# Cross attention: causal zeros set by GpSimd after the exponentials instead of mask products before them

## The reference, cut to what matters

```python
q = (Q @ wq.T).reshape(b, s, H, DH).transpose(0, 2, 1, 3)
k = (K @ wk.T).reshape(b, s, H, DH).transpose(0, 2, 1, 3)
v = (V @ wv.T).reshape(b, s, H, DH).transpose(0, 2, 1, 3)
att = jnp.einsum('bhqd,bhkd->bhqk', q, k) / jnp.sqrt(jnp.float32(DH))
causal = jnp.tril(jnp.ones((s, s), dtype=bool))
att = jnp.where(causal[None, None], att, -jnp.inf)
p = jax.nn.softmax(att, axis=-1)
out = jnp.einsum('bhqk,bhkd->bhqd', p, v)
```

## Time and profile before

| what | us |
|---|---|
| median of 3 runs | 2042.75 |
| lowest, highest | 2038.22, 2046.46 |
| span of the profiled execution | 2047.7 |
| busy in it: TensorE | 1796.9 (88%) |
| TensorE's weight loads | 1598.2 (78%) |
| VectorE | 1181.8 (58%) |
| ScalarE | 987.0 (48%) |
| GpSimd | 461.0 (23%) |
| exponentials of the cross attention, first to last start | 504.3 to 837.6 |

### The profile page before, as it was taken

The page is one execution under the profiler, slowest core; times in us unless marked ns, Lnnn a source line. Parts: engine busy times, 40 slices in busy tenths (PEclk is TensorE's granted clock), DMA queues, the critical chain, the costliest instruction groups (busy, mean ns, idle before and its releaser), DMA issues. The chain is left out here.

```text
span 2047.7 us, 39500 instructions
## 1 busy us (share of the span) xinstructions
PE 1796.9 (88%) x14845; PEld 1598.2 (78%) x14940; DVE 1181.8 (58%) x2467; ACT 987.0 (48%) x1964; POOL 461.0 (23%) x747
## 2 busy tenths in 40 slices
PE   2699999967999999578859969959999999999998
PEld 2577777756788887445549969959999999999998
DVE  2466677643676767388856869823444444444443
ACT  1367776641555555455546746623333333333331
POOL 3633443001011111134426845400000000000000
PEclk9899999986999999779979989979999999999999
DMA  5765666507877775260000033030000000000000
GB/s 165 161 142 122 132 136 140 105 25 161 178 166 161 162 161 105 91 228 1 0 1 1 1 106 97 24 117 6 10 20 10 10 10 20 10 10 10 10 16 11
DMA packets 104548, 155.87 MB, mean 76 GB/s; under 512 B 13120, under 2 KB 84800, under 8 KB 100416
## 3 DMA queue, kind: packets, MB, share of 16 engines
q1 hardware_dynamic: 99296, 149.95, 30.4%
q10 hardware_dynamic: 5120, 4.20, 1.1%
HBM read 107.97 MB, written 49.81 MB: 77 GB/s over the span
## 5 line engine op out<-in xcount | busy, mean ns | idle before, releaser
L2130 ACT ACTIVATE ffn_slots<-ps,ffn_sh 128x256 f32<-128x256 f32 x256 | 107.5, 472 | 322.7 <-PE ps L2036 322.4
L2036 PE MATMUL ps<-ffn_uT_hi,h 128*128 128x256 f32 x1024 | 245.5, 283 | 2.4 <-DVE ffn_uT_lo L2190 2.4
L2036 PE MATMUL ps<-ffn_uT_lo,h 128*128 128x256 f32 x1024 | 245.3, 283 | 0.0
L2036 PE MATMUL ps<-ffn_gT_lo,ffn_h 128*128 128x256 f32 x1024 | 243.9, 282 | 0.0
L2036 PE MATMUL ps<-ffn_gT_hi,ffn_h 128*128 128x256 f32 x1024 | 243.8, 282 | 0.0
L2036 PEld LDWEIGHTS ps<-ffn_uT_hi,h 128*128 128x128 f32 x1024 | 193.9, 189 | 2.6 <-DVE ffn_uT_lo L2190 2.6
L2036 PEld LDWEIGHTS ps<-ffn_uT_lo,h 128*128 128x128 f32 x1024 | 193.9, 189 | 0.0
L2036 PEld LDWEIGHTS ps<-ffn_gT_hi,ffn_h 128*128 128x128 f32 x1024 | 192.8, 188 | 0.0
L2036 PEld LDWEIGHTS ps<-ffn_gT_lo,ffn_h 128*128 128x128 f32 x1024 | 192.8, 188 | 0.0
L641 ACT ACTIVATE cross_probs<-ps 128x512 f32<-128x512 f32 x192 | 115.3, 602 | 108.7 <-PE ps L451 70.7
L641 ACT ACTIVATE latent_probs<-ps 128x512 f32<-128x512 f32 x192 | 115.4, 602 | 99.4 <-PE ps L451 55.9
(11 more groups left out here) (432 smaller groups left out, 5334.7 us busy)
## 6 DMA issues: line engine op xcount, KB each, us to landing
latent_split<-latent_qk_hi SPq DMA_DIRECT2D x16, 512.0 KB, 3.1
latent_split<-latent_qk_lo SPq DMA_DIRECT2D x16, 512.0 KB, 4.2
queries<-latent_split SPq DMA_DIRECT2D x32, 256.0 KB, 4.8
keys<-latent_split SPq DMA_DIRECT2D x32, 256.0 KB, 6.4
cross_split<-cross_qk_hi SPq DMA_DIRECT2D x16, 512.0 KB, 3.1
cross_split<-cross_qk_lo SPq DMA_DIRECT2D x16, 512.0 KB, 4.3
queries<-cross_split SPq DMA_DIRECT2D x32, 256.0 KB, 5.1
keys<-cross_split SPq DMA_DIRECT2D x32, 256.0 KB, 6.4
```

The source lines that it names most:

```text
L2036: last = nc.tensor.matmul(out_ap, a, b, start=start and n == 0, stop=stop and n == 1, **kw)
L2130: last = nc.scalar.activation(slots[:, p % 2, a], halved(HIDDEN_BANK + p % 2)[:, a, :], ACT.Gelu, scale=scales[:, 2 * p + a:2 * p + a + 1])
```

## The change

In the cross attention alone (`first=False`):

- `key_scores` no longer opens with the mask product; its own products start the accumulation. `query_scores` keeps its masks, so the maxima are taken over the same entries as before.
- GpSimd gets `bound_probs(i, g)`, two `affine_select` operations of 128x512 elements, in place on `probs`: the first, after the exponentials of step B, on the four diagonal 128x128 blocks of steps A and B, the second, after those of step C, on the four blocks of step C. Where the query's index is below the key's, zero is written, else the element is kept. Each counts `bounded` up.
- `weigh` waits for `bounded` instead of `ring_used`.
- GpSimd's queue in a slot becomes: `bound_probs(s - 1, 3)`, `split_context(s + 3)`, `bound_probs(s, 0)`, `row_statistics(s - 2)`, `bound_probs(s, 1)`, `bound_probs(s, 2)`.

In the diff, GpSimd's work of the first attention is only written in another way; its order there is the same.

```diff
--- before.py
+++ after.py
@@ -312,7 +312,7 @@
         q_raw, q_hi, k_raw, k_hi, qk_ready = sem("q_raw"), sem("q_hi"), sem("k_raw"), sem("k_hi"), sem("qk_ready")
         values_raw, values_ready = sem("values_raw"), sem("values_ready")
         scored, max_taken, max_split, turned, ring_used = sem("scored"), sem("max_taken"), sem("max_split"), sem("turned"), sem("ring_used")
-        shifted, weighed, evacuated = sem("shifted"), sem("weighed"), sem("evacuated")
+        shifted, weighed, evacuated, bounded = sem("shifted"), sem("weighed"), sem("evacuated"), sem("bounded")
         out_turned, normed, mixedT_raw, mixedT_hi, mixedT_ready = sem("out_turned"), sem("normed"), sem("mixedT_raw"), sem("mixedT_hi"), sem("mixedT_ready")
         latent_raw, latent_act, latent_ready = sem("latent_raw"), sem("latent_act"), sem("latent_ready")
         rope_raw, rope_biased, exchanged, roped_ready, roped_act = sem("rope_raw"), sem("rope_biased"), sem("exchanged"), sem("roped_ready"), sem("roped_act")
@@ -440,15 +440,17 @@
                     b = SECOND_RING + n % 2
                     q, k = queries[i % 3], keys[i % 3]
                     if step == "C":
-                        nc.tensor.matmul(quarters(b), ident16[:], masks[:, 1], start=True, stop=False, skip_group_check=True)
+                        if first:
+                            nc.tensor.matmul(quarters(b), ident16[:], masks[:, 1], start=True, stop=False, skip_group_check=True)
                         for m in range(4):
                             p, a = 2 * g + m // 2, m % 2
-                            last = nc.tensor.matmul(quarters(b)[:, m, :], k[:, p, a, P:S], q[:, p, P:S], start=False, stop=True, skip_group_check=True)
+                            last = nc.tensor.matmul(quarters(b)[:, m, :], k[:, p, a, P:S], q[:, p, P:S], start=not first, stop=True, skip_group_check=True)
                     else:
                         p = 2 * g + "AB".index(step)
-                        nc.tensor.matmul(halved(b)[:, :, 0:P], ident16[:], masks[:, 1, 0:2], start=True, stop=False, skip_group_check=True)
+                        if first:
+                            nc.tensor.matmul(halved(b)[:, :, 0:P], ident16[:], masks[:, 1, 0:2], start=True, stop=False, skip_group_check=True)
                         for a in range(2):
-                            last = nc.tensor.matmul(halved(b)[:, a, :], k[:, p, a, 0:P], q[:, p, :], start=False, stop=True, skip_group_check=True)
+                            last = nc.tensor.matmul(halved(b)[:, a, :], k[:, p, a, 0:P], q[:, p, :], start=not first, stop=True, skip_group_check=True)
                     last.then_inc(shifted, 1)
 
                 def turn_maxima(i, half):
@@ -463,7 +465,10 @@
                 def weigh(i, g):
 
                     q = QUADS * i + g
-                    pe.wait_ge(ring_used, ring["C", i, g] + 1)
+                    if first:
+                        pe.wait_ge(ring_used, ring["C", i, g] + 1)
+                    else:
+                        pe.wait_ge(bounded, 2 * q + 2)
                     if g == 0:
                         pe.wait_ge(values_ready, i + 1)
                     if q >= 2:
@@ -825,6 +830,14 @@
                     rows = core.X[:, i, :].rearrange("p (t d) -> p t d", d=D)
                     nc.gpsimd.tensor_tensor(rows, rows, b_out[:].to_broadcast([P, TT, D]), ALU.add).then_inc(x_biased, 1)
 
+                def bound_probs(i, g):
+                    q = QUADS * i + g
+                    two_heads = probs[:, q % 2, 0:2, :].rearrange("p n (a s) -> p (n a) s", s=S)[:, :, 0:P]
+                    four_heads = probs[:, q % 2, 2, :].rearrange("p (a s) -> p a s", s=P)
+                    for step, part in (("B", two_heads), ("C", four_heads)):
+                        pool.wait_ge(ring_used, ring[step, i, g] + 1)
+                        nc.gpsimd.affine_select(part, part, [[0, 4], [1, P]], ALU.is_ge, 0.0, base=0, channel_multiplier=-1).then_inc(bounded, 1)
+
                 if first:
                     pool.wait_ge(biases_in, BIASES)
                 for s in SLOTS:
@@ -835,12 +848,22 @@
                             heads_hi(s + 3)
                         if live(s + 4):
                             rotate(s + 4)
-                    if live(s - 2):
-                        row_statistics(s - 2)
-                    if first and live(s + 5):
-                        add_bias(s + 5)
-                    if not first and live(s + 3):
-                        split_context(s + 3)
+                        if live(s - 2):
+                            row_statistics(s - 2)
+                        if live(s + 5):
+                            add_bias(s + 5)
+                    else:
+                        if live(s - 1):
+                            bound_probs(s - 1, 3)
+                        if live(s + 3):
+                            split_context(s + 3)
+                        if live(s):
+                            bound_probs(s, 0)
+                        if live(s - 2):
+                            row_statistics(s - 2)
+                        if live(s):
+                            bound_probs(s, 1)
+                            bound_probs(s, 2)
 
             @block.vector
             def _(dve):
```

## The result

The changed kernel takes 2038.57 us (median of 20 runs, 2031.59 to 2043.15) where the kernel before takes 2045.22 us on the same chip: a ratio of 0.9970, with a 95% interval of 0.9961 to 0.9979. So it is 0.3% faster, by 6.7 us. The forecast was 2047 us, some 4 us slower; the time lies inside the range and inside the "within 0.5%", on the other side of zero.

The account below looks back on a forecast made before the run. TensorE's work was taken to bound two segments of each 22.13 us slot, a ScalarE-VectorE chain the other two. Masks -0.96, collisions +0.83 and +0.8 gave +0.67 a slot, +4 us in all: 2047 us, range 2026 to 2076.

Parts of the forecast that it names:

- X: Time of one 128x512 GpSimd select in the second attention: 0.9 us, between a 0.61 us cast and a 1.27 us subtraction.
- the ends: The four slots at the ends of the second attention, with less to collide: -1 us each, between 0 and 1.92.
- The comparison waits X - 0.07 = 0.83 us, on the chain.: Group 3 of a slot: the select starts 0.07 us before VectorE's comparison, which waits 0.83 us and delays the turn.
- No collisions: Rival: selects in the second attention fall clear of VectorE's port uses; -15.5 us, 2027 us; chance 0.26.
- With X = 0.9 both can be caught (1.5 us) ... I take 0.8.: Before group 2's turn, group 1's selects block VectorE's cast and subtraction: 0.8 us, ends 0 and 1.5.
- The masks, -0.96 us a slot.: TensorE's mask passes removed in the second attention: 1.92 us a slot, of which 0.96 arrives.
- The segments of the slot.: One slot from turn to turn: 5.98, 5.33, 5.68, 5.15 us; TensorE bounds two, a ScalarE-VectorE chain the other two.
- The sum.: Second attention: +0.67 us a slot; 12 slots +8 us, four end slots -1 us each, together +4 us.
- The long select.: Rival: from 1.2 us a select holds up `weigh(s, 0)`; at 2 us, +33 us, 2076 us; chance 0.21.
- What the profile would show.: Second attention: turn waits about 1.5 us each, comparisons near 1.4, TensorE some 25 us less busy, slot 22.8 us.

Follow-up runs that it names:

- the wide kernel: Changed kernel with the select behind step B taken over 1024 columns instead of 512; 2053.20 us, against 2043.68 us for the kernel before.
- the two kernels with the turns late: Changed kernel and kernel before, each with TensorE's turn in group 0 put behind `project_mixed` and in group 2 behind `turn_out`: 2022.38 and 2036.73 us.
- the second profile: The changed kernel profiled a second time, nothing altered; its stage takes 395.7 us, where the first profile has 398.0.

## Why the prediction went wrong, by its own steps

- *"I take X = 0.9 us, between them, since a select reads one tensor but makes an index and compares."* This is the step that failed. Measured 0.637 us. The row beside it was the cast, with one input and the same number of elements, 0.61 us; index and comparison add 0.03. I took a value near the middle of two ends, where the operation had the form of the lower one. The trace of before had the slope too: casts of 0.40 us for 256 columns and 0.61 for 512 are 0.82 ns an element. With X = 0.637 and everything else as it stands, the comparison waits 0.57 us, the selects of group 1 end at 1.2 + 4 x 0.637 + 1.47 = 5.22 and hold the cast (4.63) for 0.59, and the sum is -0.96 + 0.57 + 0.59 = +0.20 us a slot, 12 slots and the ends -1.6 us: the other sign by this term alone. The other 4 us are the 0.14 and 0.22 us by which the two collisions measured less still. The end of its range with X = 0.6 had -8 us, and 6.7 were measured. Runs of two widths, 1.063 us for 1024 and 0.637 for 512, give 0.83 ns an element, an estimated 1.0 cycle at the 1.2 GHz that the prediction took. The Trainium skill, "GPSIMD Engine Reference", section 7, has 1.03 to 2.03 cycles an element for compare and select; the trace agrees with the lower end.
- *"The comparison waits X - 0.07 = 0.83 us, on the chain."* The place, the order and the margin held (0.06 us). The size is 0.43. Even with the true X that step gives 0.57. A blocked operation is 0.15 us dearer by it than it is: comparison and select overlap from 669.83 to 670.41, 0.58 us, and 0.43 is lost; in the wide kernel 0.99 us and 0.85. The rival "No collisions" is refuted: 13 of the 14 comparisons of group 3 take 1.10 us or more.
- *"With X = 0.9 both can be caught (1.5 us) ... I take 0.8."* Measured 0.37, the cast alone; the prediction itself had 0.4 for an X of 0.6. Again X. The selects of group 1 run from 3.91 to 5.14 us behind the exponentials of (0, C), at 657.08, not from 4.5 to 6.3.
- *The masks, -0.96 us a slot.* Right: 0.97 with the masks alone removed. The two prices held too. A B step now takes 0.24 us to the next work (657.24 to 657.48) for 0.36, so 0.12 for its pass; a C step takes 0.49 us (659.54 to 660.03) for 0.72, so 0.23. The exception is step (1, B), which none of the four segments counts: 0.36 us before, 0.33 now. So TensorE gets to `weigh(s, 0)` 2.95 us behind the start of (0, C), not 2.83, and the whole that is removed is 1.64 us a slot, not 1.92. In the two kernels with the turns late, the eight A and B steps go from 2.88 to 2.05 us and the four C steps from 2.77 to 1.87, together 1.73; the last 0.09 isn't located. Here are the rows (TensorE's timeline; answer to the earlier trace rows; the last two are (1, B) before):

```profile
657.24 0.41 PE L453 MATMUL ps<-queries,keys 128*128 128x256 f32 x2
...
657.48 0.60 PE L499 MATMUL ps<-ident,state 128*128 128x128 f32 x4
...
658.26 0.40 PE L453 MATMUL ps<-queries,keys 128*128 128x256 f32 x2
658.59 0.66 PE L565 MATMUL ps<-ident,x_plus 128*128 128x128 f32 x4
...
659.54 0.56 PE L447 MATMUL ps<-queries,keys 128*128 128x128 f32 x4
...
660.03 0.64 PE L481 MATMUL ps<-cross_probs,values 128*32 128x256 f32 x8
```

```profile
662.48 0.28 PE L449 MATMUL ps<-masks,ident 128*128 128x256 bf16 x1
...
662.84 0.63 PE L560 MATMUL ps<-ident,x_plus 128*128 128x128 f32 x4
```

- *The segments of the slot.* Turn in group 0 to (0, C), 5.98, now 5.62 (651.46 to 657.08), -0.36 as forecast. From there to the turn in group 2, 5.33, now 5.56: -0.12 + 0.37 = +0.25 by the measured collision. To (3, A), 5.68, now 5.20: -0.48 as forecast. To the next turn, 5.15, now 5.57: +0.42, the comparison. Two ScalarE rows carry the ends of these (its timeline):

```profile
657.08 1.20 ACT L646 ACTIVATE cross_probs<-ps 128x512 f32<-128x512 f32 x2 [1.23 <-PE ps L447]
...
667.84 0.60 ACT L646 ACTIVATE cross_probs<-ps 128x512 f32<-128x512 f32 x1 [0.53 <-PE ps L453]
```

- *The sum.* -0.96 + 0.43 + 0.37 = -0.16 us with the collisions measured, for the +0.67 of the prediction; the slot says -0.18. Twelve slots give -2 us and the ends as forecast -4 us, together -6; 6.7 us were timed (4.3 to 8.0 by the interval). That the two come so near is in part luck, since no experiment isolates the ends. The stage in the profiles is shorter by 3.3 us at the same mean clock of 0.94, which leaves the ends 1 us; it is shorter by 5.6 in the second profile, but at a clock of 0.96. What the rest of the timed gain is stays open.
- *The long select.* Not there; `weigh` waits for GpSimd in no steady slot. The selects of group 0 end 2.46 us behind the start of (0, C), where the count gives 1.2 + 2 x 0.637 = 2.47, and TensorE comes at 2.95. It came only when each select ran twice. The four selects of group 0 then take 2.75 us (661.64 to 664.39), and by this rival's count `weigh(s, 0)` would stand for 1.2 + 2.75 - 2.83 = 1.1 us; 1.0 was measured. So this count was sound, with a condition that did not come true.
- *What the profile would show.* Waits of about 1.5 us at each turn were 1.07 and 0.70, by the smaller collisions. The comparison took 1.11 us for "near 1.4". "Some 25 us" of TensorE's busy time in the stage were 23.6.

## What to carry to other kernels

Where an operation is new to the trace, price it by the measured operation of the same form (inputs, elements, engine), and carry the range's ends through the sum separately: here 0.64 and 0.9 us, put into the same sum, give -1.6 and +4 us. When GpSimd gets work beside VectorE, look in the timeline which VectorE operations start within it and whether they stand on a chain; a move of either by one place can be worth as much as the work itself. And where an engine with the most work waits at the same place in each slot, put other work in front of that wait before anything is taken off it: 1.4 us of the 1.6 that this change freed stood at two such places, and moving two calls brought it.

## What the runs showed of the hardware

A select on GpSimd is about as cheap as a cast of the same size: 0.637 us for 128x512 f32 in place (0.61 for the cast), 1.063 us for 128x1024 (1.04 for the cast).

GpSimd and VectorE shut each other out per operation, and it goes both ways: the comparison of two SBUF inputs takes 1.11 us if it starts 0.06 us after a 0.64 us select, 1.53 after one of 1.06 us, and the select takes 1.02 us if it starts 0.15 us after the comparison. The Trainium skill, "SBUF — State Buffer", section "SBUF: two separate sides", has it as an exclusive lock that whoever starts first holds for a whole instruction. By that rule, the trace agrees. What was new is the size: VectorE's operation ends 0.53 and 0.54 us after the select does, in the two kernels, while alone it takes 0.68. By these records it loses 0.15 us less than the overlap, and a 0.18 us cast that starts 0.15 us ahead of a select's end loses nothing.

The race between select and comparison, won by 0.06 us, was won nearly always: in 13 of 14 slots here, in 13 of 14 in the second profile, and in 12 of 14 with the turns late. Both sides are released by the same ScalarE work, as the prediction had argued, and move together.
